# Linear attention in a fused decoder: the orders in which four engines issue one pipelined step

## The chip, the cores and the metric

The kernel runs on 1 core of one Trainium2 chip, in float32 throughout. The metric is the device time of the whole kernel in microseconds. The kernel before takes 4109.79 us, the median of 3 runs (4107.61 to 4110.74). The kernel is a decoder of two layers for 64 batches of 128 rows by 128 channels; the change touches the first part alone, which takes about 490 us of the span.

## The reference, cut to what matters

The first part of the decoder is `x = x + attn(layernorm(x))`, with a causal linear attention of 16 heads of 8 channels and 64 features (2 nodes x 32) for each query and key:

```python
xn   = x / maximum(norm(x), 1e-12)                    # of q and of k, per head
arg  = clip((xn @ omega) * sqrt(2 * s) - s, -20, 20)
feat = exp(arg) / sqrt(M) * sqrt(weight)              # qf, kf
...
qkv  = x @ Wqkv + bqkv
kv_cur = cumsum(k_ch[..., None] * v_ch[:, :, :, None], axis=2) + kv_state
k_cur  = cumsum(k_ch, axis=2) + k_state
out  = einsum(q_ch, kv_cur) / maximum(einsum(q_ch, k_cur), 1e-6)
return out @ Wout + bout
```

The kernel computes the same as a masked product: scores = kf qf^T for each head, times a triangle of ones, times [v, 1]; the column that comes from the 1 is the denominator.

## The kernel before, in words

**Pipeline.** Each of the 64 batches passes seven stages: NORM, QKV, KEY, FEAT, SCORE, OUT, LAST. In step n the engines work on NORM of batch n, QKV of batch n-1, and so on to LAST of batch n-6, so that one step holds one stage of seven batches. `pipeline` writes the first 8 steps out, then a loop of 14 trips of 4 steps, then 8 steps for the rest. Every engine has its own `step` function, and the order of the blocks in it is the order in which that engine issues them, written out by hand. An engine that waits for a semaphore holds up all that stands behind the wait in its own function. A stage's semaphore counts its named events; `at(name, b)` is the value that says that the event of batch b is done, and `ago=1` or `ago=2` asks for the batch one or two before.

**The operations and their short names,** with the line in the kernel before:

- TensorE: f, the features' product into the four banks of `feat` (L449); s0 and s1, the scores of the heads' two halves into the same two banks of `score` (s0 in the FEAT stage, s1 a step later in SCORE, both L432); pv, masked scores times [v, 1], into bank 0 of `feat` (L469); the projection to q, k and v (L477); y, the output projection, into bank 3 of `feat` (L485); pvT, two transposes of pv's result into bank 1 (L492); qkT (L501), attT (L515) and xnT (L522), transposes.
- VectorE: m0 and m1, the triangle mask on s0 and s1 (L555, L570); stats and mv (L563, L566); clip0 and clip1 (L579); qkv's bias (L587); x, the residual (L593); the attention rows den, rden, att (L599, L601, L604); ss and ssm, the sums of squares (L611, L614).
- ScalarE: lnn and rn, the q and k norms' inverse root (L373, L375); e0 and e1, the exponentials of `feat`'s banks 0 and 1, and 2 and 3 (L382); oT, the copy of pv out of bank 0 (L388); lnv and rstd (L393, L395); sq (L399); three copies of transposes, qkT, attT, xnT (L404, L409, L414).
- GpSimd: qkn and v (L335, L339); c, xn and xb (L346, L350, L352). SyncE loads `xin`.

**The orders before.** TensorE: f, s1, pv, projection, y, pvT, qkT, s0, attT, xnT. VectorE: m0, stats, mv, m1, clip0, clip1, bias, x, den, rden, att, ss, ssm. ScalarE: lnn, rn, e0, e1, oT, lnv, rstd, sq, qkT, attT, xnT. GpSimd: qkn, v, c, xn, xb.

**Waits that the change's steps meet.** `feat` is shared by three stages, so pv waits for e0 of the batch in FEAT, and y waits for e1 of it:

```python
if at(FEAT):
    te.wait_ge(*act_feat.at("e1", at(FEAT)))      # before y, L484
...
if at(FEAT):
    te.wait_ge(*act_feat.at("e0", at(FEAT)))      # before pv, L464
```

pv multiplies scores that were masked in the step before, so its wait for m1 (L460) is for an event one step old. s1 waits for m0 of this step (L456), m1 for s1. e0 waits for f; oT for pv; pvT for oT; den for pvT; attT for att; xnT for xn, which GpSimd makes after ScalarE's rstd; lnn for ssm; sq for the bias; ss for sq; qkT's transposes for qkn.

Of the kernel before, what the change touches and what calls it, by code (L numbers as in the profile page):

```python
# [9 lines left out]
ALU = mybir.AluOpType  # L10
ACT = mybir.ActivationFunctionType
AX = mybir.AxisListType.X
# [149 lines left out]
def flat(ap):  # L162

    return ap.rearrange("p b c -> p (b c)")
# [60 lines left out]
def linear_attention(nc, g):  # L225
# [8 lines left out]
    with ExitStack() as stack:  # L234
# [59 lines left out]
        with nc.Block() as block:  # L294
# [62 lines left out]
            @block.scalar  # L357
            def _(sc):
                sc.wait_ge(prep, 3)
                sc.activation(freq, freq, ACT.Sqrt).then_inc(prep, 1)  # L360
                sc.activation(fweight[:, 1:2], fweight[:, 0:1], ACT.Sqrt).then_inc(prep, 1)
                sc.preload_act_table_set("natural_log_exp_and_others")
                sc.activation(fbias[:, 1:2], fbias[:, 0:1], ACT.Ln).then_inc(prep, 1)
                for stage in (act_norm, act_turn, act_qkv, act_key, act_keyT, act_feat, act_out, act_att):
                    stage.start(sc)
                sc.wait_ge(prep, 8)

                def step(at):
                    b = at(KEY)
                    if b:  # L370
                        l = b.lane
                        sc.wait_ge(*vec_qkv.at("ssm", b))
                        sc.activation(ss[l][:, 1], ss[l][:, 0], ACT.Ln, scale=2.0 ** 20).then_inc(*act_key.did("lnn"))  # L373
                        sc.wait_ge(*act_key.at("lnn", b))
                        sc.activation(ss[l][:, 2], ss[l][:, 1], ACT.Exp, scale=-0.5, bias=lnscale[:]  # L375
                                      ).then_inc(*act_key.did("rn"))
                    b = at(FEAT)
                    if b:
                        sc.wait_ge(*pe_feat.at("f", b))
                        sc.wait_ge(*pe_score1.at("s1", b, ago=2))  # L380
                        for u in (0, 1):
                            sc.activation(many(ef[b.lane][:, 2 * u:2 * u + 2]), two(feat[:, 2 * u:2 * u + 2]), ACT.Exp,  # L382
                                          bias=fbias[:, 0:1]).then_inc(*act_feat.did(f"e{u}"))
                    b = at(OUT)
                    if b:
                        sc.wait_ge(*pe_out.at("pv", b))
                        sc.wait_ge(*pe_out.at("pvT", b, ago=2))
                        sc.activation(two(oT[b.lane][:]), feat[:, 0, 0:2 * T], ACT.Copy).then_inc(*act_out.did("oT"))  # L388
                    b = at(NORM)
                    if b:  # L390
                        l = b.lane
                        sc.wait_ge(*vec_norm.at("mv", b))
                        sc.activation(rstd[l][:, 0:1], mv[l][:, 1:2], ACT.Ln, bias=eps[:]).then_inc(*act_norm.did("lnv"))  # L393
                        sc.wait_ge(*act_norm.at("lnv", b))
                        sc.activation(rstd[l][:, 1:2], rstd[l][:, 0:1], ACT.Exp, scale=-0.5).then_inc(*act_norm.did("rstd"))  # L395
                    b = at(QKV)
                    if b:
                        sc.wait_ge(*vec_qkv.at("qkv", b))
                        sc.activation(sq[b.lane][:], qkv[b.lane][:, 0:2 * C], ACT.Square).then_inc(*act_qkv.did("sq"))  # L399
                    b = at(KEY)  # L400
                    if b:
                        sc.wait_ge(*pe_key.at("qkT", b))
                        sc.wait_ge(*pe_feat.at("f", b, ago=2))
                        sc.activation(two(qkT[b.lane][:]), two(turned[:, 0:2]), ACT.Copy).then_inc(*act_keyT.did("qkT"))  # L404
                    b = at(OUT)
                    if b:
                        sc.wait_ge(*pe_out.at("attT", b))
                        sc.wait_ge(*pe_last.at("y", b, ago=2))
                        sc.activation(attT[b.lane][:], turned[:, 2], ACT.Copy).then_inc(*act_att.did("attT"))  # L409
                    b = at(NORM)  # L410
                    if b:
                        sc.wait_ge(*pe_norm.at("xnT", b))
                        sc.wait_ge(*pe_qkv.at("qkv", b, ago=2))
                        sc.activation(xnT[b.lane][:], front[:, 3 * C:4 * C], ACT.Copy).then_inc(*act_turn.did("xnT"))  # L414

                pipeline(sc, g.NB, LAST + 2, step, turn=4)

            @block.tensor
            def _(te):
# [16 lines left out]
                def step(at):  # L436
# [17 lines left out]
                    if b:  # L454
                        te.wait_ge(*vec_feat.at("clip1", b))
                        te.wait_ge(*vec_mask.at("m0", b))  # L456
                        scores(b, 1).then_inc(*pe_score1.did("s1"))
                    b = at(OUT)
                    if b:
                        te.wait_ge(*vec_mask1.at("m1", b))  # L460
                        te.wait_ge(*pool_key.at("v", b))
                        te.wait_ge(*act_out.at("oT", b, ago=1))
                        if at(FEAT):
                            te.wait_ge(*act_feat.at("e0", at(FEAT)))  # L464
                        for i in (0, 1):
                            for k in (0, 1):
                                for j in range(4):
                                    rows, h = slice(32 * j, 32 * j + 32), 8 * i + 2 * j + k
                                    mm = te.matmul(feat[rows, 0, T * i:T * i + T], vpad[b.slot][:, 4 * i + j, 32 * k:32 * k + 32],  # L469
                                                   sm[b.lane][:, h // 8, h % 2, h // 4 % 2, h // 2 % 2],  # L470
                                                   start=(k == 0), stop=(k == 1))
                        mm.then_inc(*pe_out.did("pv"))
                    b = at(QKV)
                    if b:
                        te.wait_ge(*act_turn.at("xnT", b))
# [10 lines left out]
                                  ).then_inc(*pe_last.did("y"))  # L486
                    b = at(OUT)
                    if b:
                        te.wait_ge(*act_out.at("oT", b))
                        te.wait_ge(*vec_out.at("att", b, ago=1))  # L490
                        for i in (0, 1):
                            mm = te.transpose(feat[:, 1, T * i:T * i + T], oT[b.lane][:, i], g.ident[:])  # L492
                        mm.then_inc(*pe_out.did("pvT"))
                    b = at(KEY)
                    if b:
                        te.wait_ge(*pool_key.at("qkn", b))
# [3 lines left out]
                        for a in (0, 1):  # L500
                            mm = te.transpose(turned[:, a], qkv[b.lane][:, C * a:C * a + C], g.ident[:])  # L501
                        mm.then_inc(*pe_key.did("qkT"))
                    b = at(FEAT)
                    if b:
                        te.wait_ge(*vec_feat.at("clip0", b))
# [21 lines left out]
            def _(v):  # L527
# [22 lines left out]
                def step(at):  # L550
                    b = at(SCORE)
                    if b:
# [3 lines left out]
                                        score[:].rearrange("p a i t -> p (a i) t"),  # L556
                                        g.tri[:].unsqueeze(1).to_broadcast([T, 8, T]), ALU.mult
                                        ).then_inc(*vec_mask.did("m0"))
                    b = at(NORM)
                    if b:  # L560
                        l = b.lane
# [13 lines left out]
                    if b:  # L575
                        for u in (0, 1):
# [1 line left out]
                            f = many(ef[b.lane][:, 2 * u:2 * u + 2])  # L578
                            v.tensor_scalar(f, f, high[:, 0:1], low[:, 0:1], ALU.min, ALU.max  # L579
                                            ).then_inc(*vec_feat.did(f"clip{u}"))  # L580
                    b = at(QKV)
                    if b:
                        l = b.lane
                        v.wait_ge(*pe_qkv.at("qkv", b))
                        v.wait_ge(*pe_key.at("qkT", b, ago=2))
                        v.wait_ge(*pool_key.at("v", b, ago=2))
                        v.tensor_tensor(qkv[l][:], front[:, 0:3 * C], bqkv, ALU.add).then_inc(*vec_qkv.did("qkv"))  # L587
                    b = at(LAST)
                    if b:
                        one = flat(g.x[:, bass.ds(b.index, 1), :])  # L590
                        v.wait_ge(*pe_last.at("y", b))
                        v.wait_ge(*pool_norm.at("xb", b))
                        v.tensor_tensor(one, one, feat[:, 3, 0:C], ALU.add).then_inc(*vec_last.did("x"))  # L593
                    b = at(OUT)
                    if b:
                        l = b.lane
# [7 lines left out]
                        v.tensor_tensor(att[l][:].rearrange("p (h e) -> p h e", e=HD), pvT[:, :, 0:HD],  # L604
                                        rden[l][:, 1].unsqueeze(2).to_broadcast([T, H, HD]), ALU.mult
                                        ).then_inc(*vec_out.did("att"))
                    b = at(QKV)
                    if b:
                        l = b.lane
                        v.wait_ge(*act_qkv.at("sq", b))  # L610
                        v.tensor_reduce(ss[l][:, 0], sq[l][:].rearrange("p (h e) -> p h e", e=HD), AX, ALU.add  # L611
                                        ).then_inc(*vec_qkv.did("ss"))
                        v.wait_ge(*vec_qkv.at("ss", b))
                        v.tensor_scalar(ss[l][:, 0], ss[l][:, 0], 1e-24, None, ALU.max).then_inc(*vec_qkv.did("ssm"))  # L614

                pipeline(v, g.NB, LAST + 2, step, turn=4)

# [2131 lines left out]
```

## Time and profile before

| | value |
|---|---|
| median of 3 runs | 4109.79 us (4107.61 to 4110.74) |
| the profiled execution's own time | 4107.12 us |
| its span | 4105.4 us, 106579 instructions |
| TensorE matmul busy, whole span | 3860.7 us (94%) |
| VectorE busy, whole span | 3014.5 us (73%) |
| ScalarE busy, whole span | 2817.4 us (69%) |
| GpSimd busy, whole span | 1820.6 us (44%) |
| 50 to 450 us (full steps of linear attention): TensorE busy | 358.69 of 400 us, granted clock 1.00 |
| the same: VectorE, ScalarE, GpSimd busy | 330.85, 251.38, 141.88 us |

A timeline row is: start in us from the span's start, duration in us, engine, line, operation, output<-inputs, shapes, xcount, and in brackets the engine's idle time just before it with what ended it. PE is TensorE's matmul, PEld its weight load, DVE VectorE, ACT ScalarE, POOL GpSimd. Where a count is above 1 the duration covers all of them. Durations of neighbouring rows on one engine overlap a little, so the distance from start to start is what adds up. "issue" is idle time in which the engine waited for nothing that the profile shows.

### The profile page before, as it was taken

To read this page: it belongs to the slowest core of one execution; us is meant where nothing else is said; L and a number is where in the kernel's file an instruction comes from. 1 tells how busy PE (TensorE), PEld (TensorE's weight loads), DVE (VectorE), ACT (ScalarE), POOL (GpSimd) and SP (SyncE) were. 2 spreads that over 40 slices of the span, in tenths; PEclk is the share of its full clock that TensorE was granted. 3 is DMA by queue.
4 is the path that set the end of the run, shared out by engine and by line. 5 is a ranking of instruction groups with operands and counts; after the bars stand their busy time and mean duration, and the time that the engine had idled before them with its cause. 6 is when DMAs were issued, how large, how long until landed. Compare 5 with 4: busy or idle time off the path is not lost. (4 is left out here: it accounts for less than half of the span.)

```text
span 4105.4 us, 106579 instructions
## 1 busy us (share of the span) xinstructions
PE 3860.7 (94%) x33992; PEld 2986.1 (73%) x33992; DVE 3014.5 (73%) x7587; ACT 2817.4 (69%) x6420; POOL 1820.6 (44%) x1728
## 2 busy tenths in 40 slices
PE   7888899999979999898999989999999989998999
PEld 5666688888746666685666677888888866666777
DVE  6888765555569999658999955777777767776665
ACT  5666555555569999757999965777777767774333
POOL 3333222222268888526777753333333321112443
PEclk9999999999999999999999999999999999999999
DMA  0000100000000000100000010000000000000000
GB/s 18 9 9 9 49 8 6 6 6 6 15 34 9 8 8 8 27 18 10 8 8 8 14 29 27 1 0 0 0 0 0 0 3 3 3 3 6 12 12 12
DMA packets 109258, 42.46 MB, mean 10 GB/s; under 512 B 91232, under 2 KB 107872, under 8 KB 108512
## 3 DMA queue, kind: packets, MB, share of 16 engines
q1 hardware_dynamic: 109152, 41.10, 3.8%
q8 instruction: 60, 0.98, 0.1%
q14 instruction: 46, 0.38, 0.0%
HBM read 20.16 MB, written 4.19 MB: 6 GB/s over the span
## 5 line engine op out<-in xcount | busy, mean ns | idle before, releaser
L1142 POOL TENSOR_TENSOR l_rc<-l_rc,l_rs 128x1024 f32<-128x1024 f32 x128 | 303.6, 2372 | 201.5 <-DVE l_rs L1334 201.5
L1209 ACT ACTIVATE l_prob<-l_prob,l_mx 128x128 f32<-128x128 f32 x1024 | 312.1, 390 | 0.0
L1820 POOL TENSOR_TENSOR mb_steps<-w_upto,mb_dta 128x1024 f32<-128x1024 f32 x64 | 121.4, 1896 | 355.2 <-DVE mb_dta L2077 355.2
L711 POOL TENSOR_TENSOR ca_prob<-ca_prob,ca_sm 128x1232 f32<-128x1232 f32 x64 | 143.9, 2248 | 299.6 <-DVE ca_sm L877 299.6
L1234 PE MATMUL l_qk_ps<-w_local,l_hT 128*128 128x512 f32 x512 | 248.8, 609 | 13.2 <-DVE l_rs L1334 11.1
L1136 POOL TENSOR_TENSOR l_prob<-l_prob,l_sm 128x1024 f32<-128x1024 f32 x128 | 242.8, 1897 | 16.9 <-DVE l_sm L1320 16.9
L1119 POOL TENSOR_TENSOR l_rc<-l_rc,l_ss 128x1024 f32<-128x1024 f32 x128 | 243.4, 1902 | 12.5 <-POOL l_rc L1142 4.5
L1977 PE MATMUL mb_x_ps<-w_wx,mb_xT 128*128 128x256 f32 x1024 | 236.9, 385 | 0.0
L1329 DVE TENSOR_REDUCE l_ss<-l_sq 128x16 f32<-128x1024 f32 x128 | 156.1, 1219 | 77.3 <-ACT l_sq L1173 76.5
L2541 POOL TENSOR_TENSOR mo_hid<-mo_hid,mo_gate 128x1024 f32<-128x1024 f32 x64 | 121.7, 1902 | 200.0 <-DVE mo_hid L2687 200.0
L1977 PEld LDWEIGHTS mb_x_ps<-w_wx,mb_xT 128*128 128x128 f32 x1024 | 190.1, 191 | 23.1
L1242 PEld LDWEIGHTS l_att_ps<-l_probT,l_val 128*64 128x64 f32 x2048 | 109.2, 136 | 128.1 <-ACT l_probT L1160 128.1
L738 ACT ACTIVATE ca_oT<-ca_go_ps 128x1024 f32<-128x1024 f32 x64 | 65.5, 1023 | 190.2 <-PE ca_go_ps L791 190.2
L2027 DVE SCALAR_TENSOR_TENSOR mb_pre<-mb_bc_ps,w_steps,mb_pre 128x127 f32<-128x127 f32 (+2 forms) x576 | 193.0, 345 | 1.7 <-ACT mb_pre L1868 1.6
L1484 PE MATMUL m_ag_ps<-m_hT,w_gated 128*128 128x256 f32 (+1 forms) x768 | 181.2, 387 | 1.8 <-DVE m_hT L1567 1.8
L2243 POOL TENSOR_TENSOR xa_kblock<-xa_kT,xa_gmask 128x308 f32<-128x308 f32 x64 | 44.8, 700 | 293.0 <-ACT xa_kT L2283 293.0
L1271 PEld LDWEIGHTS l_score_ps<-l_kT,l_qT 64*128 64x128 f32 x2048 | 124.3, 187 | 63.5 <-issue 50.8
L1298 DVE TENSOR_TENSOR l_prob<-l_score_ps,k_local 128x1024 f32<-128x1024 f32 x128 | 156.0, 1219 | 13.1 <-PE l_score_ps L1271 9.4
L1242 PE MATMUL l_att_ps<-l_probT,l_val 128*64 128x128 f32 x2048 | 140.1, 279 | 26.8 <-ACT l_probT L1160 10.3
L2572 ACT ACTIVATE mo_hidT<-mo_turn_ps 128x512 f32<-128x512 f32 x128 | 69.5, 595 | 139.6 <-PE mo_turn_ps L2616 139.6
L1317 DVE TENSOR_REDUCE l_sm<-l_prob 128x8 f32<-128x1024 f32 x128 | 155.6, 1215 | 8.4 <-ACT l_prob L1209 4.5
L889 DVE TENSOR_TENSOR k_x<-k_x,ca_y_ps 128x128 f32 (+1 forms) x64 | 18.4, 288 | 193.7 <-PE ca_y_ps L827 193.7
(354 smaller groups left out, 12094.4 us busy)
## 6 DMA issues: line engine op xcount, KB each, us to landing
la_xin<-in_x SPq DMA_DIRECT2D x64, 64.0 KB
l_h<-lt_y SPq DMA_DIRECT2D x128, 32.0 KB
lt_quad<-lt_y SPq DMA_DIRECT2D x32, 128.0 KB
out_x<-k_x SPq DMA_DIRECT2D x64, 64.0 KB, 1.5
l_h<-lt_y SPq DMA_DIRECT2D x128, 31.8 KB
lt_quad<-lt_y SPq DMA_DIRECT2D x32, 127.0 KB
ca_ctxT<-in_ctx_T SPq DMA_DIRECT2D x128, 19.2 KB
wr_state<-in_p_state SPq DMA_DIRECT2D x1, 2438.5 KB, 11.8
```

The lines of the kernel that those rows point to most:

```text
L1119: gp.tensor_tensor(rc[l][:].rearrange("p a h e -> p (a h) e"), rc[l][:].rearrange("p a h e -> p (a h) e"), ss[l][:, 2].unsqueeze(2).to_bro ...
L1136: gp.tensor_tensor(heads, heads, sm[b.lane][:, 1].unsqueeze(2).to_broadcast([T, H, T]), ALU.mult).then_inc(*pool_prob.did("norm"))
L1142: gp.tensor_tensor(wide(rc[l][:]), wide(rc[l][:]), wide(rs[l][:]), ALU.add).then_inc(*pool_sum.did("rot"))
L1209: ex = sc.activation(p[:, a, j], p[:, a, j], ACT.Exp, bias=mx[l][:, a, j:j + 1])
L1234: mm = te.matmul(qk_ps[:, a], hT[b.slot][:], wqkv[:, a], start=True, stop=True)
L1242: mm = te.matmul(att_ps[HD * a:HD * a + HD, j], val[b.slot][:, 2 * j + a], probT[l][:, a, j], start=True, stop=True)
L1298: v.tensor_tensor(prob[b.slot][:].rearrange("p a j t -> p (a j) t"), score_ps[:].rearrange("p a j t -> p (a j) t"), g.local[:].unsqueeze(1 ...
L1317: v.tensor_reduce(sm[l][:, 0], prob[b.slot][:].rearrange("p a j t -> p (a j) t"), AX, ALU.add).then_inc(*vec_sum.did("sum"))
L1329: v.tensor_reduce(ss[l][:, 0], sq[l][:].rearrange("p a h e -> p (a h) e"), AX, ALU.add).then_inc(*vec_rot.did("ss"))
L1484: mm = te.matmul(ag_ps[half][0:M[c], c, N * a:N * a + N], w1[:, a, 128 * c:128 * c + M[c]], hT[b.lane][:, N * half:N * half + N], start=Tr ...
L1977: mm = te.matmul(x_ps[:, DI * k:DI * k + DI], xT[l][:, at_j:at_j + T], wx[:, k, j], start=(j == 0), stop=(j == TAPS - 1))
L2027: v.scalar_tensor_tensor(out=out, in0=bc_ps[:, T * i + there.start:T * i + there.stop], scalar=cw[:, k, 2 + SHIFTED[i][1], TAPS - 1 - back ...
```

## The change

No operation is added, removed or resized; all four `step` functions but GpSimd's and SyncE's are reordered:

- TensorE now issues f, s1, **projection, y**, pv, **qkT**, pvT, s0, attT, xnT.
- VectorE now issues m0, **ss, ssm**, stats, mv, m1, clip0, clip1, **den, rden, att**, x, **bias**. ss and ssm belong to the KEY stage now, one step after the bias of the same batch.
- ScalarE now issues **e0**, lnn, rn, **e1**, oT, lnv, rstd, qkT, attT, xnT, **sq**.

```diff
 # ScalarE
+                    b = at(FEAT)
+                    if b:
+                        sc.wait_ge(*pe_feat.at("f", b))
+                        sc.wait_ge(*pe_score1.at("s1", b, ago=2))
+                        sc.activation(many(ef[b.lane][:, 0:2]), two(feat[:, 0:2]), ACT.Exp,
+                                      bias=fbias[:, 0:1]).then_inc(*act_feat.did("e0"))
                     b = at(KEY)
...
                     b = at(FEAT)
                     if b:
-                        sc.wait_ge(*pe_feat.at("f", b))
-                        sc.wait_ge(*pe_score1.at("s1", b, ago=2))
-                        for u in (0, 1):
-                            sc.activation(many(ef[b.lane][:, 2 * u:2 * u + 2]), two(feat[:, 2 * u:2 * u + 2]), ACT.Exp,
-                                          bias=fbias[:, 0:1]).then_inc(*act_feat.did(f"e{u}"))
+                        sc.activation(many(ef[b.lane][:, 2:4]), two(feat[:, 2:4]), ACT.Exp,
+                                      bias=fbias[:, 0:1]).then_inc(*act_feat.did("e1"))
...
-                    b = at(QKV)
-                    if b:
-                        sc.wait_ge(*vec_qkv.at("qkv", b))
-                        sc.activation(sq[b.lane][:], qkv[b.lane][:, 0:2 * C], ACT.Square).then_inc(*act_qkv.did("sq"))
...
+                    b = at(QKV)
+                    if b:
+                        sc.wait_ge(*vec_qkv.at("qkv", b))
+                        sc.activation(sq[b.lane][:], qkv[b.lane][:, 0:2 * C], ACT.Square).then_inc(*act_qkv.did("sq"))
 # TensorE, behind s1
+                    b = at(QKV)
+                    if b:
+                        te.wait_ge(*act_turn.at("xnT", b))
+                        te.wait_ge(*vec_qkv.at("qkv", b, ago=1))
+                        te.matmul(front[:, 0:3 * C], xnT[b.lane][:], wqkv, start=True, stop=True
+                                  ).then_inc(*pe_qkv.did("qkv"))
+                    b = at(LAST)
+                    if b:
+                        te.wait_ge(*act_att.at("attT", b))
+                        te.wait_ge(*vec_last.at("x", b, ago=1))
+                        if at(FEAT):
+                            te.wait_ge(*act_feat.at("e1", at(FEAT)))
+                        te.matmul(feat[:, 3, 0:C], attT[b.lane][:], wout, start=True, stop=True
+                                  ).then_inc(*pe_last.did("y"))
                     b = at(OUT)
...
                         mm.then_inc(*pe_out.did("pv"))
...
                         mm.then_inc(*pe_key.did("qkT"))
+                    b = at(OUT)
+                    if b:
+                        te.wait_ge(*act_out.at("oT", b))
+                        te.wait_ge(*vec_out.at("att", b, ago=1))
+                        for i in (0, 1):
+                            mm = te.transpose(feat[:, 1, T * i:T * i + T], oT[b.lane][:, i], g.ident[:])
+                        mm.then_inc(*pe_out.did("pvT"))
 # VectorE
+                    b = at(KEY)
+                    if b:
+                        l = b.lane
+                        v.wait_ge(*act_qkv.at("sq", b))
+                        v.tensor_reduce(ss[l][:, 0], sq[l][:].rearrange("p (h e) -> p h e", e=HD), AX, ALU.add
+                                        ).then_inc(*vec_qkv.did("ss"))
+                        v.wait_ge(*vec_qkv.at("ss", b))
+                        v.tensor_scalar(ss[l][:, 0], ss[l][:, 0], 1e-24, None, ALU.max).then_inc(*vec_qkv.did("ssm"))
                     b = at(NORM)
...
```

In VectorE's function the blocks LAST (x) and QKV (bias) move, unchanged, from between clip1 and den to behind att, in this order.

## Rows read from the trace of the kernel before

**Rows 1.** Timeline of VectorE: m0 at the start of two trips, four steps apart.

```profile
112.05 1.22 DVE L555 TENSOR_TENSOR la_sm<-la_score,k_tri 128x1024 f32<-128x1024 f32 x1 [0.42 <-issue]
...
141.10 1.23 DVE L555 TENSOR_TENSOR la_sm<-la_score,k_tri 128x1024 f32<-128x1024 f32 x1 [0.41 <-issue]
```

**Rows 2.** Timeline, all engines, one full step inside a trip.

```profile
271.83 1.15 PE L449 MATMUL la_feat<-la_qkT,la_w 32*128 32x256 f32 x16
...
272.11 0.22 ACT L373 ACTIVATE la_ss<-la_ss 128x32 f32<-128x32 f32 x1
272.37 0.32 ACT L375 ACTIVATE la_ss<-la_ss,la_lnscale 128x32 f32<-128x32 f32 x1
...
273.05 2.12 ACT L382 ACTIVATE la_ef<-la_feat,la_fbias 128x1024 f32<-128x1024 f32 x2 [0.36 <-PE la_feat L449]
...
274.27 1.23 DVE L570 TENSOR_TENSOR la_sm<-la_score,k_tri 128x1024 f32<-128x1024 f32 x1 [0.92 <-PE la_score L432]
274.27 0.84 PEld L469 LDWEIGHTS la_feat<-la_sm,la_vpad 128*32 128x32 f32 x32 [0.24 <-issue]
...
275.52 0.38 ACT L388 ACTIVATE la_oT<-la_feat 128x256 f32<-128x256 f32 x1 [0.35 <-PE la_feat L469]
275.75 0.51 PEld L485 LDWEIGHTS la_feat<-la_w,la_attT 128*128 128x128 f32 x2
...
276.18 0.26 PEld L492 LDWEIGHTS la_feat<-k_ident,la_oT 128*128 128x128 f32 x2
...
276.40 0.25 PEld L501 LDWEIGHTS la_turned<-k_ident,la_qkv 128*128 128x128 f32 x2
276.40 0.79 POOL L346 TENSOR_TENSOR la_off<-la_xin,la_mv 128x128 f32<-128x128 f32 x1 [2.59 <-ACT la_rstd L395]
...
277.35 0.40 POOL L350 TENSOR_TENSOR la_xn<-la_off,la_rstd 128x128 f32<-128x128 f32 x1 [0.16 <-POOL la_off L346]
...
278.30 0.41 DVE L611 TENSOR_REDUCE la_ss<-la_sq 128x32 f32<-128x256 f32 x1
...
278.44 0.33 PE L515 MATMUL la_turned<-k_ident,la_att 128*128 128x128 f32 x1 [0.46 <-DVE la_att L604]
...
278.73 0.33 PE L522 MATMUL la_front<-k_ident,la_xn 128*128 128x128 f32 x1
...
278.84 1.23 DVE L555 TENSOR_TENSOR la_sm<-la_score,k_tri 128x1024 f32<-128x1024 f32 x1
...
278.98 1.15 PE L449 MATMUL la_feat<-la_qkT,la_w 32*128 32x256 f32 x16
```

**Rows 3.** Groups by line, 50 to 500 us: busy us, mean ns, idle before.

```profile
L587 DVE TENSOR_TENSOR la_qkv<-la_front,la_w 128x384 f32<-128x384 f32 x58 | 32.0, 551 | 0.0
...
L593 DVE TENSOR_TENSOR k_x<-k_x,la_feat 128x128 f32 (+1 forms) x63 | 17.6, 280 | 3.3 <-PE la_feat L485 3.3
```

**Rows 4.** Timeline, last steps of the stage, where FEAT or KEY has run out.

```profile
478.08 0.20 PEld L492 LDWEIGHTS la_feat<-k_ident,la_oT 128*128 128x128 f32 x2 [0.27 <-ACT la_oT L388]
...
478.45 0.97 PEld L432 LDWEIGHTS la_score<-la_ef 64*128 64x128 f32 x16 [0.17 <-DVE la_ef L579]
...
481.13 1.00 PEld L432 LDWEIGHTS la_score<-la_ef 64*128 64x128 f32 x16 [1.05 <-issue]
...
482.25 0.81 PEld L469 LDWEIGHTS la_feat<-la_sm,la_vpad 128*32 128x32 f32 x32
...
483.40 0.38 ACT L388 ACTIVATE la_oT<-la_feat 128x256 f32<-128x256 f32 x1 [2.82 <-PE la_feat L469]
...
483.83 0.20 PEld L492 LDWEIGHTS la_feat<-k_ident,la_oT 128*128 128x128 f32 x2 [0.28 <-ACT la_oT L388]
...
485.15 0.14 PEld L515 LDWEIGHTS la_turned<-k_ident,la_att 128*128 128x128 f32 x1 [1.11 <-DVE la_att L604]
```

**Rows 5.** Timeline of TensorE at the start of a loop trip.

```profile
111.43 0.32 PE L522 MATMUL la_front<-k_ident,la_xn 128*128 128x128 f32 x1
112.31 1.15 PE L449 MATMUL la_feat<-la_qkT,la_w 32*128 32x256 f32 x16 [0.56 <-issue]
```

More of the change, by code:

```diff
@@ L457, in step @@
                         scores(b, 1).then_inc(*pe_score1.did("s1"))
[L458 to L472, printed above, removed]
                     b = at(QKV)
@@ L488, in step @@
                     if b:
-                        te.wait_ge(*act_out.at("oT", b))
-                        te.wait_ge(*vec_out.at("att", b, ago=1))
-                        for i in (0, 1):
-                            mm = te.transpose(feat[:, 1, T * i:T * i + T], oT[b.lane][:, i], g.ident[:])
-                        mm.then_inc(*pe_out.did("pvT"))
+                        te.wait_ge(*vec_mask1.at("m1", b))
+                        te.wait_ge(*pool_key.at("v", b))
+                        te.wait_ge(*act_out.at("oT", b, ago=1))
+                        if at(FEAT):
+                            te.wait_ge(*act_feat.at("e0", at(FEAT)))
+                        for i in (0, 1):
+                            for k in (0, 1):
+                                for j in range(4):
+                                    rows, h = slice(32 * j, 32 * j + 32), 8 * i + 2 * j + k
+                                    mm = te.matmul(feat[rows, 0, T * i:T * i + T], vpad[b.slot][:, 4 * i + j, 32 * k:32 * k + 32],
+                                                   sm[b.lane][:, h // 8, h % 2, h // 4 % 2, h // 2 % 2],
+                                                   start=(k == 0), stop=(k == 1))
+                        mm.then_inc(*pe_out.did("pv"))
                     b = at(KEY)
@@ L580, in step @@
                                             ).then_inc(*vec_feat.did(f"clip{u}"))
[L581 to L593, printed above, removed]
                     b = at(OUT)
@@ L606, in step @@
                                         ).then_inc(*vec_out.did("att"))
+                    b = at(LAST)
+                    if b:
+                        one = flat(g.x[:, bass.ds(b.index, 1), :])
+                        v.wait_ge(*pe_last.at("y", b))
+                        v.wait_ge(*pool_norm.at("xb", b))
+                        v.tensor_tensor(one, one, feat[:, 3, 0:C], ALU.add).then_inc(*vec_last.did("x"))
                     b = at(QKV)
@@ L609, in step @@
                         l = b.lane
[L610 to L614, printed above, removed]
+                        v.wait_ge(*pe_qkv.at("qkv", b))
+                        v.wait_ge(*pe_key.at("qkT", b, ago=2))
+                        v.wait_ge(*pool_key.at("v", b, ago=2))
+                        v.tensor_tensor(qkv[l][:], front[:, 0:3 * C], bqkv, ALU.add).then_inc(*vec_qkv.did("qkv"))
                 pipeline(v, g.NB, LAST + 2, step, turn=4)
```

## The prediction, made before the changed kernel was run

> **What bounds the kernel now.** I first took the busy shares by engine in the stretch of full steps (the table ahead): TensorE is busy 90% of it at granted clock 1.00, so there is little to win under it, but 10% of idle that a reorder may touch. Then the timeline of one step. m0 starts at 112.05 and, four steps on, at 141.10 [rows 1]: a trip is 29.05 us, 7.26 a step. Inside a trip, f to f is 278.98 - 271.83 = 7.15 [rows 2], so the branch at the trip's end adds 29.05 - 4 x 7.15 = 0.45.
>
> What releases what in that step: VectorE idles 0.92 until s1 is done, then runs m1 and everything else without a gap to m0; m0 releases s1, s1 releases m1. That is one ring, with ss and ssm in it. TensorE idles 0.46 for att in front of attT. Both engines are thus nearly closed: the reader is to see in [rows 2] that m0 (278.84) and f (278.98) start together, 0.40 and 0.54 behind attT (278.44).
>
> **The change part by part.** No operation changes, so each edit is worth only what it does to waits. I write times from f's start.
>
> *ss and ssm into VectorE's wait for s1.* They stood from 278.30 to 278.84, 0.54 us [rows 2], and go into an idle stretch of 0.92. Taken alone this shortens VectorE's ring by 0.54. What they push is stats, mv and so rstd; before, c started 276.40, long after mv, since rstd stands behind oT in ScalarE's order. So it costs nothing there.
>
> *den, rden, att ahead of x and bias.* x and bias take 0.28 and 0.55 [rows 3]. They used to run while pvT was being made; att is now earlier only if pvT is there. bias moves right in front of m0; sq and the next projection, which need it, are a step later and have spare: sq is issued behind xnT's copy and ss is only wanted behind m0 (1.23).
>
> *Projection and y ahead of pv.* The stated idea is to fill the wait for the mask. But pv multiplies scores masked in the step before: in [rows 2] pv's weights load at 274.27, the very moment at which m1 of this step starts. There is no mask to wait for. pv waits for e0, and e0 is just done: 273.05 + half of 2.12 is 274.11. What now stands before pv is y, and y waits for **e1**, because both use bank 3 of the features. TensorE is in order, so pv inherits that wait.
>
> *e0, lnn, rn, e1.* In the old order e0 starts at 1.22 and the pair takes 2.12, so e1 would be done at 3.34. Now lnn and rn stand between: lnn to rn is 272.37 - 272.11 = 0.26, and rn to what follows it between 0.22 (its 0.32 less the 0.10 by which such rows overlap, my estimate from 2.12 against twice a single exponential) and 0.32; I take 0.22. e1 ends at 1.22 + 2.12 + 0.26 + 0.22 = 3.82 [rows 2].
>
> *What TensorE does meanwhile.* Before, pv started at 274.27 - 271.83 = 2.44. In its place the projection starts. pv and projection together took 275.75 - 274.27 = 1.48, of which pv's loads alone were 0.84, so the projection takes at most 0.64 and y's turn comes by 3.08. It stands still for 0.74 or more, until 3.82 plus the 0.05 that a release takes (oT's end 483.40 + 0.38 = 483.78, pvT 483.83) [rows 4]: y starts at 3.87.
>
> *The new ring from there.* y to pv: two passes after a stall were 478.45 - 478.08 = 0.37 [rows 4]; the nearest others are 276.40 - 276.18 = 0.22 and y's own 276.18 - 275.75 = 0.43 behind the wide projection [rows 2]. I take 0.37: pv at 4.24, not 2.44. pv to pvT, through oT, is 483.83 - 482.25 = 1.58 [rows 4]; the projection and y used to lie in that gap, and now only qkT does, whose input is ready (rn ends near 2.8, and qkn is one GpSimd operation). pvT at 5.82. From pvT to attT there are two ways. Through den, rden and att: 485.15 - 483.83 = 1.32. Through s0 on TensorE: 0.37 (478.08 to 478.45) plus 1.12 for sixteen score products (481.13 to 482.25), 1.49 [rows 4]. The longer holds: attT at 7.31. attT, xnT, f are 0.54 as before [rows 2], so the next f starts at **7.85**.
>
> As a check by differences: pv is 1.80 later; pv to attT was 278.44 - 274.27 = 4.17 and is now 1.58 + 1.49 = 3.07, 1.10 less; 1.80 - 1.10 = +0.70 = 7.85 - 7.15.
>
> *Who else could be last.* GpSimd: oT at 4.24 + 1.15 = 5.39; oT to c 276.40 - 275.52 = 0.88; c to xn 0.95; xn 0.40; release 0.05: xnT at 7.67, against 7.60 from attT. It can add 0.07 [rows 2, 4]. VectorE: att ends by 7.09, x and bias at full length end by 7.92, so m0 starts at most 0.07 behind f where it now leads by 0.14; s1 is then up to 0.14 late, and the 0.74 of standing at y swallows it. So what VectorE gains is not on the path that sets the end.
>
> *The trip's end.* xnT to f is 112.31 - 111.43 = 0.88 there against 0.25 inside a trip [rows 2, 5]: 0.63 on TensorE, of which the old ring felt 0.45. TensorE's path is now the ring, so I charge all 0.63.
>
> A rule of the skill bears on y to pv. The trace: attT's weight load starts at 485.15, behind the wait for att and not ahead of it [rows 4]. The Trainium skill, "TensorE: Matmul & The Clock Gate", in its section "Step-by-step: what each phase is for", says that TensorE may pull weight loads ahead of matmuls in flight while matmuls keep their order. If it pulled pv's loads past y's wait, y to pv would be nearer 0.22, and the time 0.15 x 61 = 9 us lower; the row speaks for no pull past a semaphore, so I keep 0.37.
>
> **Sum.** Per trip 4 x 0.70 + 0.63 - 0.45 = 2.98 us; 14 trips: 41.7. Steps 6, 7 and 64 to 66, outside the loop but with FEAT and LAST both active: 5 x 0.70 = 3.5. Together +45.2. The profiled execution took 4107.12 (span 4105.4): 4152.3. The median of the runs is 2.7 above that execution, so 4155.
>
> Bounds. Low: y to pv 0.22, attT through att alone (1.32), the next f then held by xn at about 7.6, +0.45 a step, and a trip's end that is hidden in the waits (nothing where the old had 0.45): 14 x 1.35 + 5 x 0.45 = 21 us, 4131. High: rn 0.32, y 0.43, xn 0.07 late and 0.1 for releases that no row shows: +0.93 a step, 14 x 3.90 + 5 x 0.93 = 59 us, 4169.
>
> **The rivals.**
> - *VectorE's ring decides, faster.* The 0.54 of ss and ssm leaves the ring, up to the 0.46 that TensorE idles now: -0.46 x 61 = -28 us, 4082. For it: VectorE has no other gap than the 0.92, and m1 follows s1 in every step. Against it: it needs e1 done before y's turn at 3.08, and e1 ends at 3.82. It decides only if I have misread y's wait or the two exponentials run much sooner.
> - *The two effects cancel.* TensorE's new wait hides the branch and y's pass, and the loss at y is half what I think, 0.3 a step against 0.3 gained: within 8 us of 4110. Nothing in the rows halves it, since each link is an issue order or a wait.
> - *Slower still.* With TensorE busy 81% (90% x 7.26 / 8.01) the granted clock, 1.00 now (2.4 GHz), is at its other level (1.2 GHz) for part of the time; a mean of 0.9 lengthens the products on the ring (f, pv, s0, about 3.4 us) by about 0.3 a step: 18 us more, 4173.
> - *The change does what it says* (the projection fills a wait for the mask): there is no such wait, and this earns nothing by itself.
>
> **How the numbers follow.** Forecast with its bounds 85%; slower still 6%; cancel 4%; VectorE's ring 5%. Measurements of this kernel tell about 0.2% (8 us) from no change. Faster 0.05, same 0.04, slower 0.91. Range 4128 to 4175, the bounds widened to the clock's case.
>
> **What would show it.** In the new trace, per step: y starts right behind e1's end, released by ScalarE, with TensorE idle 0.7 to 1.0 in front of it; pv follows y and starts 4.2 behind f; oT to pvT leaves a second idle of about 0.4; f to f near 7.85; VectorE idle about 0.3 before m1 and over 1 us before den. It is wrong if y starts by 3.3 behind f, if e1 does not end its wait, or if f to f stays under 7.3.

## The result, and the profile after

The changed kernel takes 4191.34 us, the median of 4 runs (4189.71 to 4193.35), against 4109.49 us before (here the median of 4 runs, in the table ahead of 3): a ratio of 1.0203, 95% interval 1.0191 to 1.0215. It is slower, as forecast, but by 82 us where 45 was forecast, and 4191 lies above the range's end of 4175.

In the windows of the trace after (columns: stretch, its length, busy us of each engine, granted clock, DMA share, GB/s) the full steps show the same clock as before and an emptier TensorE, 327.54 us of 400 against 358.69:

```profile
50.00:450.00 400.00, 327.54 (x4209) 222.11 (x4212) 299.56 (x653) 209.98 (x514) 112.65 (x235) 1.00 0.03 8
```

VectorE's m0 at the start of two trips, which answers [rows 1], gives 34.22 us a trip where it was 29.05: 8.56 a step, +5.17 a trip.

```profile
89.45 1.23 DVE L558 TENSOR_TENSOR la_sm<-la_score,k_tri 128x1024 f32<-128x1024 f32 x1
...
123.67 1.23 DVE L558 TENSOR_TENSOR la_sm<-la_score,k_tri 128x1024 f32<-128x1024 f32 x1
```

One full step inside a trip, which answers [rows 2] (timeline after; L452 is f, L435 s1, L473 y, L486 pv, L504 pvT, L518 attT, L525 xnT, L617 the bias):

```profile
98.82 1.15 PE L452 MATMUL la_feat<-la_qkT,la_w 32*128 32x256 f32 x16
...
99.89 1.16 PE L435 MATMUL la_score<-la_ef 64*128 64x128 f32 x16
...
100.03 1.11 ACT L373 ACTIVATE la_ef<-la_feat,la_fbias 128x1024 f32<-128x1024 f32 x1 [0.52 <-PE la_feat L452]
...
101.04 0.22 ACT L379 ACTIVATE la_ss<-la_ss 128x32 f32<-128x32 f32 x1
...
101.30 0.32 ACT L381 ACTIVATE la_ss<-la_ss,la_lnscale 128x32 f32<-128x32 f32 x1
101.52 1.10 ACT L385 ACTIVATE la_ef<-la_feat,la_fbias 128x1024 f32<-128x1024 f32 x1
...
102.24 1.77 DVE L590 TENSOR_SCALAR la_ef<-la_ef,la_high,la_low 128x1024 f32<-128x1024 f32 x2
102.28 0.46 POOL L339 TENSOR_TENSOR la_vpad<-la_qkv,k_ones 128x128 f32<-128x128 f32 x1
...
102.67 0.49 PE L473 MATMUL la_feat<-la_w,la_attT 128*128 128x128 f32 x2 [0.77 <-ACT la_ef L385]
...
103.09 1.08 PE L486 MATMUL la_feat<-la_sm,la_vpad 128*32 128x128 f32 x32
...
104.31 0.38 ACT L391 ACTIVATE la_oT<-la_feat 128x256 f32<-128x256 f32 x1 [1.70 <-PE la_feat L486]
...
104.75 0.44 PE L504 MATMUL la_feat<-k_ident,la_oT 128*128 128x128 f32 x2 [0.21 <-ACT la_oT L391]
...
105.23 0.17 DVE L597 TENSOR_SCALAR la_rden<-la_feat 128x16 f32<-128x16 f32 x1 [1.22 <-PE la_feat L504]
...
105.81 0.29 DVE L602 TENSOR_TENSOR la_att<-la_feat,la_rden 128x128 f32<-128x128 f32 x1
...
106.21 0.33 PE L518 MATMUL la_turned<-k_ident,la_att 128*128 128x128 f32 x1
106.32 0.56 DVE L617 TENSOR_TENSOR la_qkv<-la_front,la_w 128x384 f32<-128x384 f32 x1
...
106.80 1.21 DVE L558 TENSOR_TENSOR la_sm<-la_score,k_tri 128x1024 f32<-128x1024 f32 x1
...
106.94 0.33 PE L525 MATMUL la_front<-k_ident,la_xn 128*128 128x128 f32 x1 [0.39 <-DVE la_qkv L617]
...
107.19 0.71 PE L452 MATMUL la_feat<-la_qkT,la_w 32*128 32x256 f32 x8
```

The step is 107.19 - 98.82 = 8.37 us, where it was 7.15. TensorE has two long waits in it. y stands 0.77 us for e1, and pv follows it at 4.27 behind f where it was 2.44. And xnT stands 0.39 us for the **bias**: it follows attT by 0.73, where it was 0.29. The waits in total over 50 to 480 us (engine, line, what it waited for: us, times, longest) name the same two on TensorE:

```profile
DVE la_rden L597 <- PE la_feat L504: 63.2, 50, 1.4
...
PE la_feat L473 <- ACT la_ef L385: 40.5, 51, 0.9
...
DVE la_sm L581 <- PE la_score L435: 31.3, 51, 1.0
...
PE la_front L525 <- DVE la_qkv L617: 20.3, 50, 0.7
```

VectorE idles 63.2 us in front of den, where it had no gap before, and 31.3 in front of m1: its new gap is where the forecast put it. The granted clock of 1.00 and TensorE's 82% also answer the forecast's rival "slower still": at just about the busy share that it assumed (81%), the clock did not fall in the full steps.

The stage's share: the next stage's first matmul is at 572.50 in the trace after and at 490.77 in that before, 81.7 us later, as much as the median changed (81.9). The two profiled executions are 86.2 apart, so they differ by 4.5 behind this stage too, where the kernels are the same; the runs of the changed kernel alone spread over 3.6. Of it 14 x 5.17 = 72.4 lies in the trips, and 5.8 behind the last f (22.55 us to the next stage, 16.73 before); which leaves 3.5 for the steps outside the loop.

### The profile page after: what moved, and what is told of

Read it like the earlier page. It is cut to its first block and busy times, and to the rows that moved or that the text cites. A ratio compares the mean times of both kernels' runs of the same rounds, so it can differ in the third digit from the quotient of the medians.

```text
span 4191.6 us, 106565 instructions
## 1 busy us (share of the span) xinstructions
PE 3897.2 (93%) x33992; PEld 2982.9 (71%) x33992; DVE 3037.4 (72%) x7587; ACT 2814.9 (67%) x6420; POOL 1810.6 (43%) x1728
```

## The experiments

All are judged by the median; "before" in each was 4108.6 to 4108.8 us.

**e1: y back behind pv.** In the changed kernel TensorE's LAST block, y with its waits, moves:

```diff
-                        te.matmul(feat[:, 3, 0:C], attT[b.lane][:], wout, start=True, stop=True
...
                         mm.then_inc(*pe_out.did("pv"))
...
+                        te.matmul(feat[:, 3, 0:C], attT[b.lane][:], wout, start=True, stop=True
```

> The changed kernel with one block of TensorE's order put back: y behind pv instead of ahead of it. Theory A (pv inherits y's wait for e1): pv starts about 2.7 behind f (it was 4.27), pvT about 4.4, att ends about 5.8, and then the bias, last on VectorE, holds xnT until about 6.45: f to f near 6.75 inside a trip against 8.42 changed and 7.15 before. Total near 4085 us, so faster than the kernel before by some 0.5%. Theory B (the loss sits in the reordered VectorE and ScalarE functions, y's place is a bystander): f to f stays above 8, total within 15 us of 4191.

4110.49 us, ratio 1.0002 (0.9993 to 1.0011). One block gives back 81 of the 82 us, so theory A's cause stands. Its size was off by 25 us: the timeline of e1 (L478 pv, L488 y, L518 attT, L617 bias, L525 xnT) shows pv at 3.0 behind f (f at 250.84), behind the projection's 0.84, and not at 2.7, and attT bound by s0 and xnT by the bias, 0.65 behind attT. The gain that theory A expected over the kernel before is not there, but y's place alone decides between 4191 and 4110:

```profile
253.85 1.08 PE L478 MATMUL la_feat<-la_sm,la_vpad 128*32 128x128 f32 x32
...
254.86 0.49 PE L488 MATMUL la_feat<-la_w,la_attT 128*128 128x128 f32 x2
...
256.97 0.33 PE L518 MATMUL la_turned<-k_ident,la_att 128*128 128x128 f32 x1
257.00 0.56 DVE L617 TENSOR_TENSOR la_qkv<-la_front,la_w 128x384 f32<-128x384 f32 x1
...
257.62 0.33 PE L525 MATMUL la_front<-k_ident,la_xn 128*128 128x128 f32 x1 [0.32 <-DVE la_qkv L617]
```

**e2: e1 straight behind e0,** lnn and rn behind both, all else as changed.

```diff
+                        sc.activation(many(ef[b.lane][:, 2:4]), two(feat[:, 2:4]), ACT.Exp,
...
                         sc.activation(ss[l][:, 1], ss[l][:, 0], ACT.Ln, scale=2.0 ** 20).then_inc(*act_key.did("lnn"))
...
-                        sc.activation(many(ef[b.lane][:, 2:4]), two(feat[:, 2:4]), ACT.Exp,
```

> The changed kernel with e1 straight behind e0 and lnn, rn behind both. Theory A (e1's end is on the ring that sets the step): e1 ends 0.48 earlier (two ScalarE distances, 0.25 and 0.23), y and all behind it too, so 0.48 x 61 = 29 us less: 4162. Theory B (something later, such as rn, qkn or xn, holds the step): less than 8 us change.

4163.71 us, ratio 1.0134 (1.0119 to 1.0150): 28 us less, as theory A says. The end of e1 is on the ring (the closed chain of waits that sets the step), and lnn and rn in front of it cost 28 of the 82 us.

**e3: the bias alone back ahead of den.**

```diff
+                        v.tensor_tensor(qkv[l][:], front[:, 0:3 * C], bqkv, ALU.add).then_inc(*vec_qkv.did("qkv"))
...
                         v.tensor_tensor(att[l][:].rearrange("p (h e) -> p h e", e=HD), pvT[:, :, 0:HD],
...
-                        v.tensor_tensor(qkv[l][:], front[:, 0:3 * C], bqkv, ALU.add).then_inc(*vec_qkv.did("qkv"))
```

> The changed kernel with the bias alone put back ahead of den on VectorE. Theory A (the part of the loss that the forecast missed is xnT's wait for the bias, since both use the bank front): xnT follows attT by 0.28 again instead of 0.64 to 0.78, f to f 8.42 - 0.42 = 8.0, 61 x 0.42 = 26 us less: 4166. Theory B (xnT would be held by xn or attT's copy just as late): less than 8 us change. Theory C (att is made later by the bias ahead of it): no gain or a loss.

4164.60 us, ratio 1.0137 (1.0121 to 1.0152): 27 us less. In its timeline the bias (L598) runs while VectorE has nothing else, and xnT follows attT by 0.31 with no wait:

```profile
91.55 0.55 DVE L598 TENSOR_TENSOR la_qkv<-la_front,la_w 128x384 f32<-128x384 f32 x1
...
94.03 0.32 PE L518 MATMUL la_turned<-k_ident,la_att 128*128 128x128 f32 x1
...
94.34 0.32 PE L525 MATMUL la_front<-k_ident,la_xn 128*128 128x128 f32 x1
```

**e4: the kernel before, only ss and ssm moved** into the wait for s1.

```diff
+                    b = at(KEY)
...
+                        v.tensor_reduce(ss[l][:, 0], sq[l][:].rearrange("p (h e) -> p h e", e=HD), AX, ALU.add
...
                         v.bn_stats(stats[l][:], xin[l][:]).then_inc(*vec_norm.did("stats"))
...
-                    b = at(QKV)
...
-                        v.tensor_reduce(ss[l][:, 0], sq[l][:].rearrange("p (h e) -> p h e", e=HD), AX, ALU.add
```

> The kernel before with only ss and ssm moved into VectorE's wait for s1. Theory A (VectorE's ring through m0 is only just behind a second ring f, s1, m1, clips, bias, x, den, att, attT, xnT, f, which ss and ssm are not on): f to f falls from 7.15 to about 7.0, since s1 can follow f by 1.07 instead of 1.21; 0.14 x 61 = 8 us less, 4101. Theory B (the forecast's rival: the whole 0.46 that TensorE idles is won): 28 us less, 4082.

4111.62 us, ratio 1.0007 (0.9998 to 1.0016). Neither theory: no gain at all. lnn and rn are ahead of e0 here and now wait for the later ssm: in its timeline lnn starts at 251.43 and e0 only at 251.92, 2.01 behind f (249.91) where it was 1.22. pv, which waits for e0, starts at 253.16, 3.25 behind f where it was 2.48.

**e5: the kernel before, only projection and y ahead of pv.**

```diff
+                        te.matmul(front[:, 0:3 * C], xnT[b.lane][:], wqkv, start=True, stop=True
...
+                        te.matmul(feat[:, 3, 0:C], attT[b.lane][:], wout, start=True, stop=True
...
                         mm.then_inc(*pe_out.did("pv"))
...
-                        te.matmul(front[:, 0:3 * C], xnT[b.lane][:], wqkv, start=True, stop=True
...
-                        te.matmul(feat[:, 3, 0:C], attT[b.lane][:], wout, start=True, stop=True
```

> The kernel before with only TensorE's projection and y moved ahead of pv. Theory A (y's wait for e1 costs by itself): here e0 and e1 are adjacent, e1 ends 3.34 behind f, y 3.40, pv 3.82, pvT 5.48, attT 6.95, and the bias, early on VectorE, holds nothing: f to f 7.5 against 7.15; with the trip's end +23 to +27 us, 4132 to 4136. Theory B (it needs the other edits to hurt): within 8 us of 4109.

4136.05 us, ratio 1.0067 (1.0051 to 1.0082): 27 us slower by the place of the projection and y alone, as theory A says. This price and those of e2 and e3, 27 + 28 + 27, add up to the 82 us of the whole change. In its timeline the pair of exponentials ends 3.33 behind f, and y (L470) starts 0.05 later, pv (L483) at 3.80 and attT at 7.14:

```profile
93.51 1.15 PE L449 MATMUL la_feat<-la_qkT,la_w 32*128 32x256 f32 x16
...
94.72 2.12 ACT L382 ACTIVATE la_ef<-la_feat,la_fbias 128x1024 f32<-128x1024 f32 x2 [0.28 <-PE la_feat L449]
...
96.89 0.49 PE L470 MATMUL la_feat<-la_w,la_attT 128*128 128x128 f32 x2 [0.23 <-ACT la_ef L382]
...
97.31 1.08 PE L483 MATMUL la_feat<-la_sm,la_vpad 128*32 128x128 f32 x32
...
100.65 0.33 PE L515 MATMUL la_turned<-k_ident,la_att 128*128 128x128 f32 x1
```

**e6: the changed kernel with TensorE's whole order put back.** Its diff is the TensorE part of the change, reversed.

> The changed kernel with TensorE's whole order put back (VectorE's and ScalarE's new orders stay). Theory A: pv at 2.4 behind f, projection and y fill oT's gap, pvT 4.35, s0 4.98; att ends about 5.8, attT 6.1, and the bias, last on VectorE, ends 6.46 and holds xnT: f to f about 6.76 against 7.15 before: some 20 to 25 us faster than the kernel before, 4085 to 4089. Theory B (VectorE's and ScalarE's new orders are themselves worth nothing): 4109 within 8.

4103.27 us, ratio 0.9989 (0.9980 to 0.9998). Faster than before, but by 5 us and not 20 to 25: f to f is 7.05 to 7.12 inside a trip, not 6.76. Its trace has xnT waiting for the bias, 22.7 us in 56 times over 50 to 450 us, and clips of 0.91 us where they were 0.81; e7 takes the first away, e11 the second.

**e7: as e6, the bias between rden and att.**

```diff
                         v.reciprocal(rden[l][:, 1], rden[l][:, 0]).then_inc(*vec_out.did("rden"))
+                        v.tensor_tensor(qkv[l][:], front[:, 0:3 * C], bqkv, ALU.add).then_inc(*vec_qkv.did("qkv"))
...
                         v.tensor_tensor(att[l][:].rearrange("p (h e) -> p h e", e=HD), pvT[:, :, 0:HD],
...
-                        v.tensor_tensor(qkv[l][:], front[:, 0:3 * C], bqkv, ALU.add).then_inc(*vec_qkv.did("qkv"))
```

> As e6, with the bias between rden and att on VectorE, so that xnT no longer waits behind x and the bias. Theory A: att starts 5.8 instead of 5.5, attT stays at s0's end, 6.12, xnT 6.4, f to f about 6.66: 4079 to 4085, 6 us below e6. Theory B (att is later by the bias's 0.5 and attT follows it): no gain against e6.

4094.08 us, ratio 0.9964 (0.9950 to 0.9978): 9 us below e6. In its trace xnT no longer waits for the bias. It still lies 9 us or more above the 4079 to 4085 of theory A; e11 shows where that went.

**e8 and e10: the kernel before, ss and ssm moved, and e0 first on ScalarE;** in e8 then lnn, rn, e1, in e10 then e1, lnn, rn.

> The kernel before with ss and ssm moved into the wait for s1, as e4, and e0 ahead of lnn and rn, so that e0 no longer stands behind lnn's wait for ssm. Theory A (a second ring f, s1, m1, clips, bias, x, den, att, attT, xnT is 0.14 shorter than VectorE's): f to f 7.0, 8 us less than before, 4101. Theory B (moving ss and ssm frees the 0.46 that TensorE idles): 4082. Theory C (nothing gained): 4109 within 4.

> e8 (the kernel before, ss and ssm moved, e0 first) with e1 straight behind e0 too. Theory A (e8 lost because lnn and rn delay e1 and clip1 waits 0.24 for it, and the second ring through att has no ss and ssm in it to lose): f to f 7.23 - 0.24 = 6.99, against 7.15 before: 4100. Theory B (moving ss and ssm frees the 0.46 that TensorE idled): 4082.

4115.70 us (1.0018, 1.0009 to 1.0027) and 4124.58 us (1.0037, 1.0024 to 1.0051): both slower than before, and e10, in which e1 comes earliest, the slower. So a late e1 is not what costs e8 its gain: I had read a wait of clip1 for e1 into clip1's later start, and over 50 to 450 us the waits of e8, e9 and e10 list none.

**e9: e7 with e1 straight behind e0.**

> e7 (TensorE's old order, the bias between rden and att) with e1 straight behind e0, lnn and rn behind both. Theory A (in e7 lnn and rn delay e1, clip1 waits 0.24 for it, and so den is late): clip1 follows clip0 without a gap, den 4.9 behind f instead of 5.0 to 5.1, att ends 6.1, f to f 6.67 against 6.86 in e7: 11 us less, about 4083. Theory B (TensorE or GpSimd holds the step at 6.8, or rn is now too late for qkT): 4094 within 4.

4102.21 us, ratio 0.9984 (0.9975 to 0.9993): 8 us slower than e7 where theory A had 11 faster.

What e8 to e10 share is seen in the groups by line, 50 to 450 us (columns as in [rows 3]): the clips, then GpSimd's qkn and v. Before:

```profile
L579 DVE TENSOR_SCALAR la_ef<-la_ef,la_high,la_low 128x1024 f32<-128x1024 f32 x111 | 85.0, 808 | 0.0
...
L335 POOL TENSOR_TENSOR la_qkv<-la_qkv,la_ss 128x256 f32<-128x256 f32 x55 | 34.5, 628 | 101.6 <-ACT la_ss L375 101.6
...
L339 POOL TENSOR_TENSOR la_vpad<-la_qkv,k_ones 128x128 f32<-128x128 f32 x55 | 25.0, 455 | 0.0
```

In e8:

```profile
L590 DVE TENSOR_SCALAR la_ef<-la_ef,la_high,la_low 128x1024 f32<-128x1024 f32 x109 | 95.1, 912 | 0.0
...
L335 POOL TENSOR_TENSOR la_qkv<-la_qkv,la_ss 128x256 f32<-128x256 f32 x55 | 34.7, 631 | 213.9 <-ACT la_ss L381 213.9
L339 POOL TENSOR_TENSOR la_vpad<-la_qkv,k_ones 128x128 f32<-128x128 f32 x55 | 32.8, 596 | 0.0
```

In e9:

```profile
L590 DVE TENSOR_SCALAR la_ef<-la_ef,la_high,la_low 128x1024 f32<-128x1024 f32 x112 | 103.2, 963 | 0.0
...
L339 POOL TENSOR_TENSOR la_vpad<-la_qkv,k_ones 128x128 f32<-128x128 f32 x56 | 50.3, 899 | 0.0
...
L335 POOL TENSOR_TENSOR la_qkv<-la_qkv,la_ss 128x256 f32<-128x256 f32 x56 | 45.8, 818 | 230.3 <-ACT la_ss L385 230.3
```

The same instructions on the same shapes: a clip takes 808 ns before, 912 in e8 and 963 in e9; v takes 455, 596 and 899; qkn 628, 631, 818. With rn behind e0 (e8) or e1 (e9), qkn and v fall beside the clips, and both engines' instructions stretch. In e9 and e10 there is a second suspect, rn itself: the weight load of qkT waits 0.2 us a step for qkn (10.0 us in 56 times in e9), so how their loss divides is open. In e7 and e8 that wait is missing, and the next two runs start from these.

**e11 and e12: v ahead of GpSimd's wait for rn,** in e7 and in e8. v needs only the bias's result.

```diff
+                        gp.wait_ge(*vec_qkv.at("qkv", b))
+                        gp.wait_ge(*pe_out.at("pv", b, ago=4))
+                        gp.tensor_tensor(by_head(vpad[b.slot])[:, :, :, 0:HD], split(qkv[l][:, 2 * C:3 * C]),
...
                         gp.wait_ge(*act_key.at("rn", b))
...
-                        gp.wait_ge(*pe_out.at("pv", b, ago=4))
-                        gp.tensor_tensor(by_head(vpad[b.slot])[:, :, :, 0:HD], split(qkv[l][:, 2 * C:3 * C]),
```

> e7 with GpSimd's v ahead of its wait for rn instead of behind qkn, so that v no longer runs beside the clips. Theory A (clip0 and clip1 take 1.67 to 1.77 instead of 1.53 together because GpSimd works on SBUF at the same time): clips mean 0.91 falls to 0.81 to 0.83, v from 0.60 to 0.46, den 0.15 to 0.2 earlier, f to f 6.86 to about 6.68: 10 to 12 us less than e7, 4082 to 4084. Theory B (the clips are long because clip1 waits for e1): clips unchanged, 4094 within 4.

> e8 (the kernel before, ss and ssm moved, e0 first) with v ahead of the wait for rn. Theory A (contention with GpSimd cost e8 what the shorter ring gained): f to f 7.23 less 0.2 is 7.03, against 7.15 before: 4102 to 4105. Theory B (moving ss and ssm frees all that TensorE idled): 4082. Theory C (the clips wait for e1): 4116 as e8.

e11 takes 4081.37 us, ratio 0.9934 (0.9920 to 0.9948); e12 4103.58 us, 0.9988 (0.9979 to 0.9997). Both as theory A says, e11 by 0.6 us more. The clips are back at 0.81 in both, by the groups of e11 and then of e12:

```profile
L591 DVE TENSOR_SCALAR la_ef<-la_ef,la_high,la_low 128x1024 f32<-128x1024 f32 x118 | 90.2, 806 | 0.0
```

```profile
L591 DVE TENSOR_SCALAR la_ef<-la_ef,la_high,la_low 128x1024 f32<-128x1024 f32 x112 | 85.5, 805 | 0.0
...
L341 POOL TENSOR_TENSOR la_qkv<-la_qkv,la_ss 128x256 f32<-128x256 f32 x55 | 34.7, 631 | 191.6 <-ACT la_ss L382 191.6
...
L337 POOL TENSOR_TENSOR la_vpad<-la_qkv,k_ones 128x128 f32<-128x128 f32 x56 | 25.4, 454 | 0.0
```

**e11 is the fastest version,** by 27 us against before and 110 against the changed one; f to f is 6.61 to 6.83 inside a trip.

**e13: e3, with y behind pv in the steps without a FEAT stage.**

```diff
-                    if b:
+                    if b and at(FEAT):
...
                         mm.then_inc(*pe_out.did("pv"))
+                    b = at(LAST)
+                    if b and not at(FEAT):
...
+                        te.matmul(feat[:, 3, 0:C], attT[b.lane][:], wout, start=True, stop=True
```

> e3 with y put behind pv in the last steps alone, those without a FEAT stage. Theory A (the rest of the miss, 4165 against a forecast of 4155, is for two thirds in the last steps, where y ahead of pv must wait for ScalarE's copy of attT, and pv behind it): from the last f to the next stage's first matmul 24.6 us falls to about 17 to 18, 6 to 7 us less than e3: 4158. Theory B (the last steps are long for another reason): 4165 within 3.

4160.88 us, ratio 1.0132 (1.0116 to 1.0147), with runs from 4157.63 to 4166.81: 4 us below e3, but the intervals overlap, so the median alone does not settle it. The traces do for the place: last f to the next stage is 18.0 us (523.96 to 541.97), in e3 24.6 (521.98 to 546.56). Much of that is the clock. These are the windows from the last f to the next stage, over the same operations, in the kernel before, the changed one, e3 and e13 (columns as above):

```profile
474.04:490.77 16.73, 11.63 (x178) 8.36 (x178) 8.97 (x19) 4.40 (x10) 0.04 (x1) 1.00 0.01 2
```

```profile
549.95:572.50 22.55, 14.93 (x179) 10.63 (x178) 9.22 (x19) 4.41 (x10) 0.04 (x1) 0.76 0.01 1
```

```profile
521.98:546.56 24.58, 17.11 (x179) 12.06 (x178) 9.23 (x19) 4.41 (x10) 0.04 (x1) 0.62 0.00 1
```

```profile
523.96:541.97 18.01, 11.60 (x178) 8.36 (x178) 9.23 (x19) 4.40 (x10) 0.04 (x1) 1.00 0.01 2
```

The granted clock is 0.62 in e3, so much of the stretch is at 1.2 GHz, and 1.00 in e13. Of the 6.6 us between them TensorE's busy time, for the same matmuls, is 17.11 - 11.60 = 5.5, and only 1.1 is more standing still. Of the changed kernel's 5.8 us over the kernel before, 3.3 is busy time at a granted clock of 0.76, and 2.5 is standing still. y's place is not the only thing that the clock follows there: e11, with y behind pv as before, has 0.89 in this stretch, while e6 and e7 have 1.00. Each is one trace, and why they differ is open.

## Why the prediction was right in kind and too small

**Right: y's wait for e1.** Forecast y 3.87 behind f, pv 4.24, pvT 5.82, attT 7.31. Measured in the step shown: 3.85, 4.27, 5.93, 7.39. e1 and e5 show the cause from both sides, e2 the part of lnn and rn in it. There is no wait for the mask, as said.

The second idle, in front of pvT, is 0.21 by the matmul's row (forecast about 0.4).

**Right: no pull of pv's load past y's wait.** y to pv is 0.42, nearer to the 0.37 taken than to the 0.22 of the other case, in which pv's loads go past the wait. The rule on weight loads of the Trainium skill ("TensorE: Matmul & The Clock Gate", "Step-by-step: what each phase is for"), that they are pulled ahead of matmuls in flight, is thus not seen to reach past a semaphore here: pv's first load starts with its matmul, at 103.09.

**Wrong: "attT, xnT, f are 0.54 as before".** This is the step that failed. The sum took xnT as bound by attT or by xn, and not by VectorE's bias. But xnT waits for the bias of the step's QKV batch (L521 of the kernel before), because both use the bank `front`; before, the bias ended 1.3 us ahead of xnT (276.85 + 0.55 against 278.73), so no row of the old trace shows the wait. Moved to VectorE's end, the bias ends after att. Measured attT to f: 0.98 in the step shown; e3 prices it at 27 us of the 36 missed. The prediction does list who needs the bias, but only sq and the next projection, both a step later; xnT, in the same step, is missing. Its own numbers would have shown the wait: it has the bias end by 7.92, which puts xnT at 7.97 instead of 7.60, the next f at 8.22, and the whole, by my estimate, 0.37 x 61 = 23 us higher, at 4178.

**Undersized by a little:** y to pv 0.42 (taken 0.37) and pv to pvT 1.66 (taken 1.58), 0.13 a step, of which y's and attT's slightly earlier links give 0.05 back.

**Wrong: nothing charged behind the last f.** There y has no e1 to wait for, but it waits for attT's copy of the step before, and pv, which did not, now stands behind it. This stretch is 5.8 us longer in the changed kernel, 2.5 of it more standing still and 3.3 a lower granted clock (the windows at e13). e13 shows the place: with y behind pv there, the stretch of e3 shrinks by 6.6.

**The account closes by the traces.** The stage grew by 81.7 us against 45.2 forecast, 36.5 more. The trips missed by 14 x (5.17 - 2.98) = 30.7, of which the bias is 25.6 (a trip is 34.22 us, in e3 32.39) and the small links the rest; the stretch behind the last f is the other 5.8. The steps outside the loop took 3.5, as forecast. The trip's end was charged 0.18 too much: the step over it is 8.89 us against 8.37 to 8.53 for the others, and was 7.79 against 7.00 to 7.14, so it grew by 1.10 and they by 1.35.

**Slips in the sums,** none of which would have caught the miss: the high bound counts 0.93 a step where its four parts add 0.33 to 0.70, which is 1.03, and ends near 4175 instead of 4169; in the low bound xnT at 7.52 gives the next f at 7.77, not 7.6, so the bound is nearer 4141; and a mean clock of 0.9 lengthens 3.4 us by 0.38, not 0.3.

**Wrong as a rival: -28 us from ss and ssm.** With m0 earlier, s1 follows f by 1.07 instead of 1.21, and that is all: the ring through m1, clips, bias, x, den, att, attT, xnT, f has neither ss nor ssm in it. e12, which also has e0 first on ScalarE and v first on GpSimd, gives -5 us; e4, with ss and ssm moved alone, none.

## What to carry to other kernels

When an instruction is moved later in one engine's order, list who waits for its semaphore on every other engine, waits that never show in the trace included: a wait that was always met early is invisible until its event becomes late. When one is moved ahead of another on an in-order engine, the second inherits all its waits; here a matmul for a bank that ScalarE empties last was put in front of one for the bank emptied first. And price a freed slot by the ring that is next, not by the idle time in front of it.

## What was not expected of the hardware

VectorE's clip (128x1024, SBUF to SBUF, one tensor operand) and GpSimd's operations lengthen when they meet: 0.81 to 0.91 and 0.96 us a clip, 0.46 to 0.90 for v. e11 and e12 show it by moving v alone: 12.7 and 12.1 us for the whole kernel. The kernel before has such a meeting too, but there GpSimd alone pays: c starts while the clips run and takes 0.72 on average, in the changed kernel, behind them, 0.40, while the clips keep their 0.81. The Trainium skill, "SBUF — State Buffer", section "SBUF: two separate sides", says that GpSimd and a VectorE instruction in a two-port mode hold one shared pair of ports in turn, each for the whole of an instruction. The numbers agree in that either engine can be the one that is delayed; that the clip runs in such a mode, and that the later instruction stands still for the whole of the other, no run here shows. In the changed kernel itself the clips are as stretched (1.77 for the pair at 102.24, 1.53 before), but VectorE then idles 1.22 us for pvT, so there it costs nothing.

The other is the clock: in the last steps, where TensorE waits through one serial chain, the granted clock is 0.76 of full in the changed kernel and 0.62 in e3, and pv's 32 products, 1.08 us in the steps, take up to 1.94 us there. The kernel before and e13 go through a like chain at 1.00.
